# A decoder layer with routed experts: projections as three rounded products of split operands, quantised layers without diagonal matrices, routing in four pieces, and another order

## The chip, the core and the metric

The kernel runs on one core of one Trainium2 chip. The metric is the time of one execution on the device in microseconds (us). TensorE (PE) multiplies, VectorE (DVE), ScalarE (ACT) and GpSimd (POOL) work element by element, and SyncE (SP) issues the transfers between the device memory and the on-chip memory. The engines run side by side and wait for one another by semaphores. TensorE's clock has two levels, 1.2 and 2.4 GHz; a row of the profile gives the granted share of the higher one.

## The reference

Input x is four sequences of 512 tokens of width 512, all float32. One layer is three parts, each added to its input and normalised.

```
def attention(x, Wqkv, bqkv, Wo, bo):            # 16 heads of 32
    kqv = (x @ Wqkv + bqkv).reshape(b, s, 3, 16, 32)
    q, k, v = kqv[:, :, 0], kqv[:, :, 1], kqv[:, :, 2]
    scores = einsum('bsnh,btnh->bnst', k, q) / sqrt(32)
    scores = triu(scores) - 10000 * tril(ones, -1)
    attn = softmax(scores, axis=2)
    return einsum('bnkq,bknh->bqnh', attn, v).reshape(b, s, 512) @ Wo + bo

def quant_linear(x, w):                          # once per batch and layer
    s = sqrt(max|x| over tokens / max|w| over rows)      # one per input column
    xs, ws = x / s, w * s
    xq = round(xs / (max|xs| per row / 127)); wq = round(ws / (max|ws| per row / 127))
    return xq @ wq.T * x_scale * w_scale.T

x = layernorm(x + attention(x))
g, u = split(quant_linear(x, fside[b])); x = layernorm(x + quant_linear(silu(g) * u, ctx[b]))
x = layernorm(x + sum over 4 of 16 experts of their weighted FFN + 2 shared FFNs)
```

The routing takes the 2 best of 4 groups of experts and in them the 4 best experts, by ranks.

## The kernel before

**Stages.** A table of words, `SEQ`, gives the order of steps; every engine walks the same table and does its own part of each step. A first pass (from 0 to 148 us in the trace) does the attention (A) of batch 0. A loop of three turns does A of batch a together with the quantised layers and the routing (B) of batch a-1. Each turn ends with the output projection `wo`. A last pass does B of batch 3, mixed with halves of the shared experts' tiles (`half`), of which 8 tiles of 16 are merged into it. The other shared tiles follow, with the placing of tokens between them, then 71 or more tiles of the routed experts, and a last normalisation.

**Words of the table.** `xt` transposes x. `qk:n` and `v:n` are the projections, `max` the row maxima of the scores, `rows` turns the maxima into a row, `scores` the scores, exponentials and masks, `weigh` the weighted sum, `bc` divides by the denominators, `wo` is the output projection. For a quantised layer n, `wtr` and `xtr` transpose weights and inputs so that DVE can take column maxima, `s` makes the column scales, `ws` and `xs` bring a scale to all partitions and scale, `wq` and `xq` quantise, `wb` brings the weight scales to all partitions, `wqt` and `xqt` transpose, `h` multiplies. `ln1`, `a2` and `ln2` close the parts; `x2t`, `lg`, `lgt` and `route` are the routing.

**Products.** A projection step (`product`, L1097) is four float32 products of 512 columns, one for each 128 rows of the input width; the trace has two records for each. Weights lie in `room`, loaded once. The product by the diagonal matrices `dg` that DVE builds (L1609, L1617) brings a scale to all partitions (L1097 as well). The score products take q and k as a rounded part and a rest (`qhl`), which go through the device memory (`scr_d`) into stacked tiles `qst` and `kst`: SP stores them after each odd `qk`, waits, and loads six pieces of 256 KB (L680 to L690). `rows` sends two small rows, `nmh` and `nml`, into `qst` (L694, L695), and every fourth `scores` waits for them.

**Banks.** Three PSUM banks (`psR`) serve all one-bank steps in turn: a step waits until the step three tickets back has been read (`take_bank`). So the engine that reads a step's result also sets when PE may go on.

**What the queues hold.** SP's transfers go out in the order of its program. Per turn they are: fside and ctx of batch b (L653, L654), `xr` of batch a after the first normalisation of b (L660), `xt` of the next batch (L673), then the stores and loads of q and k, the rows, and `x2`.

## Time and profile before

| | us |
|---|---|
| median of 3 runs | 1494.71 |
| lowest and highest | 1491.39, 1494.90 |
| the profiled execution, as timed | 1494.37 |
| its span in the trace | 1492.6 |
| what lies around the span | 1.8 |

| engine | busy us | share |
|---|---|---|
| PE (TensorE) | 1337.6 | 90% |
| PEld (its weight loads, beside it) | 993.9 | 67% |
| DVE | 889.9 | 60% |
| ACT | 412.3 | 28% |
| POOL | 390.3 | 26% |

The shares are means over stages with different limits. The first row of a stage to read is the one that gives all engines in that stretch; then the waits of PE inside it. Busy time of PE is modelled, with matmuls that overlap.

### The profile page before, as it was taken

Reading aid. Unit: us, or ns where it says so; the run is one execution under the profiler, and the core shown is the slowest. Engines: PE = TensorE matmul, PEld = TensorE weight load, DVE = VectorE, ACT = ScalarE, POOL = GpSimd, SP = SyncE. Lnnn points to the kernel's source line nnn. Section 1 sums busy time; section 2 is a strip of 40 time slices with the busy share of each in tenths; the row PEclk is TensorE's granted clock in tenths of the full one; section 3 lists DMA queues with packets and bytes.
Section 4 is the critical chain, followed back from the end, with each engine's and each line's share of the span. In section 5 each row is a group of like instructions: output and inputs, shape, how many; then the busy total and the mean of one; then the engine's idle time right before and its main releaser. Section 6 shows DMA issues by size and latency. Waiting matters only on the chain.

```text
span 1492.6 us, 24655 instructions
## 1 busy us (share of the span) xinstructions
PE 1337.6 (90%) x7331; PEld 993.9 (67%) x7339; DVE 889.9 (60%) x1580; ACT 412.3 (28%) x628; POOL 390.3 (26%) x478
## 2 busy tenths in 40 slices
PE   7988998999999999689978997999999999879991
PEld 3553455445444554377867887899999999768891
DVE  2442787668866986786646876334343455455534
ACT  1131133313340234121120003223222334343423
POOL 1131012200230023000000671334343344243432
PEclk9989998999999999889998999999999999999996
DMA  8430533224422533203110012645464456868447
GB/s 281 131 93 34 155 97 89 72 100 126 114 71 73 153 105 128 90 14 110 64 57 29 29 43 64 164 75 130 86 140 76 86 131 138 236 159 247 80 78 248
DMA packets 90110, 163.98 MB, mean 110 GB/s; under 512 B 8544, under 2 KB 29536, under 8 KB 89968
## 3 DMA queue, kind: packets, MB, share of 16 engines
q1 hardware_dynamic: 73168, 122.88, 26.6%
q0 software_dynamic: 16816, 39.59, 14.3%
q8 instruction: 58, 0.95, 0.3%
q14 instruction: 68, 0.56, 0.1%
HBM read 113.42 MB, written 49.02 MB: 109 GB/s over the span
## 4 chain that ended last, share of the span: by engine, by line
PE 67%; DVE 13%; DMA 8%; issue 5%; ACT 3%; POOL 2%; SPq 1%; DVEq 1%; ACTq 0%; POOLq 0%
PE psR L1097 12%; PE psUA L1005 12%; PE psUB L1005 12%; PE psY L1012 9%; PE psR L1012 5%; PE psR L1173 3%; PE psOT L1204 3%; PE psST L1187 3%; PE psR L1111 2%; PE psTX L988 2%; DMA kst<-scr_d 2%; PE psTH L1021 2%; DMA room<-in_L_ffn_w_dram 2%; DMA qst<-nml 1%; DVE w_s L1261 1%
## 5 line engine op out<-in xcount | busy, mean ns | idle before, releaser
L1005 PE MATMUL psUA<-w_s,xgT 128*128 (+1 forms) x1284 | 246.5, 342 | 2.0 <-DVE xgT L1381 1.7
L1005 PE MATMUL psUB<-w_s,xgT 128*128 (+1 forms) x1284 | 226.8, 325 | 0.0
L1005 PEld LDWEIGHTS psUA<-w_s,xgT 128*128 128x128 f32 x1284 | 215.7, 197 | 9.7 <-issue 8.1
L1005 PEld LDWEIGHTS psUB<-w_s,xgT 128*128 128x128 f32 x1284 | 213.1, 191 | 0.0
L829 POOL DMA_INDIRECT sx_d<-yg,dst_i x74 | 119.5, 1614 | 304.5 <-ACT yg L908 265.7
L868 ACT ACTIVATE silg<-psUA 128x352 f32<-128x352 f32 x107 | 49.6, 464 | 444.0 <-PE psUB L1005 444.0
L1012 PE MATMUL psY<-w_s,hgT 128*128 (+3 forms) x621 | 161.4, 404 | 0.3 <-issue 0.3
L791 POOL TENSOR_SCALAR_AFFINE_SELECT pT<-pT 128x128 f32<-128x128 f32 (+1 forms) x192 | 68.7, 377 | 342.0 <-ACT pT L946 341.8
L1390 DVE SCALAR_TENSOR_TENSOR hg<-silg,cws,psUB 128x352 f32<-128x352 f32 x75 | 43.4, 579 | 176.3 <-ACT silg L868 176.3
L1571 DVE TENSOR_REDUCE nm<-psR 128x1 f32<-128x128 f32 (+3 forms) x256 | 112.4, 486 | 38.7 <-PE psR L1175 34.7
L1012 PEld LDWEIGHTS psY<-w_s,hgT 128*128 128x128 f32 (+1 forms) x621 | 113.4, 190 | 22.3 <-issue 0.5
L1097 PE MATMUL psR<-xT,room 128*128 128x512 f32 x256 | 117.4, 605 | 2.4 <-ACT xT L918 2.4
L1396 DVE CAST hgT<-psTH 128x384 fp32r<-128x384 f32 x107 | 59.5, 556 | 95.5 <-PE psTH L1021 95.1
L816 POOL DMA_INDIRECT xg<-x_d,src_i x77 | 98.4, 1279 | 52.9 <-issue 22.2
L1261 DVE TENSOR_TENSOR w_s<-room,w_s (+2 forms) x54 | 88.1, 1667 | 32.7 <-ACT w_s L859 31.9
L946 ACT ACTIVATE pT<-psST 128x512 f32<-128x512 f32 (+1 forms) x128 | 83.9, 703 | 85.5 <-PE psST L1187 84.6
L1173 PE MATMUL psR<-kst,qst 96*128 96x256 f32 (+2 forms) x256 | 91.4, 428 | 15.9 <-DMA kst<-scr_d 6.2
L1021 PE MATMUL psTH<-ident,hg 128*128 128x128 f32 x321 | 55.1, 281 | 39.9 <-DVE hg L1390 20.9
L1097 PEld LDWEIGHTS psR<-xT,room 128*128 128x128 f32 x256 | 48.1, 193 | 59.4 <-issue 54.5
L1012 PE MATMUL psR<-w_s,hgT 128*128 (+1 forms) x333 | 86.8, 405 | 1.0 <-issue 1.0
L1204 PE MATMUL psOT<-pT,v_s 128*32 128x256 f32 (+3 forms) x512 | 80.3, 440 | 7.4 <-POOL pT L791 7.4
L859 ACT CAST w_s<-room (+2 forms) x54 | 73.6, 1404 | 48.2 <-DVE room L1547 21.9
(221 smaller groups left out, 1923.3 us busy)
## 6 DMA issues: line engine op xcount, KB each, us to landing
room<-in_L_ffn_w_dram SPq DMA_DIRECT2D x32, 704.0 KB, 6.1
scr_d<-qhl SPq DMA_DIRECT2D x32, 512.0 KB, 3.7
qst<-scr_d SPq DMA_DIRECT2D x48, 256.0 KB, 3.9
kst<-scr_d SPq DMA_DIRECT2D x48, 256.0 KB, 5.8
room<-in_L_ffn_w_dram SPq DMA_DIRECT2D x16, 512.0 KB, 7.3
xt<-in_x_dram SPq DMA_DIRECT2D x5, 1024.0 KB, 7.2
xr<-in_x_dram SPq DMA_DIRECT2D x4, 1024.0 KB, 5.4
breg<-in_fside_BxS2xS_dram SPq DMA_DIRECT2D x4, 1024.0 KB, 7.6
```

The lines of the kernel that those rows point to most:

```text
L816: pool.indirect_dma_start(xg[:, par, :], None, x2_d, bass.IndirectOffsetOnAxis(ap=src_i[:, j:j + 1], axis=0)).then_inc(s_gat[par], 16)
L829: pool.indirect_dma_start(sx_d, bass.IndirectOffsetOnAxis(ap=dst_i[:, j:j + 1], axis=0), yg[:, par, :], None, compute_op=ALU.add).then_inc ...
L859: act.copy(hi, raw).then_inc(s_whi, 1)
L946: act.activation(pT[:, h % 4, lo:hi], psST[:, lo:hi], ACT.Exp, scale=SCALE).then_inc(s_exp, 1)
L1005: mm = pe.matmul(t[:, 0:F], xgT[:, par, a_, c * P:(c + 1) * P], w[:, buf, b_, c, :], start=(c == 0 and n == 0), stop=(c == C - 1 and n == ...
L1012: mm = pe.matmul(psy[:, :], hgT[0:kn, a_, k * P:(k + 1) * P], w2_s[0:kn, buf, b_, k, :], start=(first and k == 0 and n == 0), stop=(last_ ...
L1021: mm = pe.transpose(psTH[0:kn, k * P:(k + 1) * P], hg[:, k0:k0 + kn], ident[:, :])
L1097: mm = pe.matmul(out_, l, r, start=(n == 0), stop=(n == len(pairs) - 1))
L1173: pe.matmul(t[:, 0:w], qst[0:96, i, j, q * P:(q + 1) * P], kst[0:96, i, j, 0:w], start=True, stop=False)
L1204: pe.matmul(psOT[HD * j:HD * (j + 1), kb * P:S], v_s[:, kb, h * HD:(h + 1) * HD], pT[:, h % 4, cols], start=(kb == 0), stop=(kb == ST - 1) ...
L1261: dve.tensor_tensor(lo, raw, hi.bitcast(F32), ALU.subtract).then_inc(s_wlo if n in UP else s_w2lo, 1)
L1571: done(dve.tensor_reduce(nm[:, n, q:q + 1], at.bank(x, q)[:, 0:(q + 1) * P], AX.X, ALU.max, negate=True))
```

## The change

**Projections.** Weights of q, k, v and o are now kept as a rounded part and a rest (type fp32r), and so are x (`xT` has two halves) and the attention's output (`ohl`). A projection step is twelve rounded products instead of four float32 ones: high by high, high by low, low by high for each 128 rows. The split of a weight is made once, in the first pass: raw weights are loaded into tiles of B that are free then (`WRAW`), ACT copies the rounded part, DVE subtracts (`USES` says before which step). The tile `late_w` holds the q and k weights of groups 2 and 3 and later those of `wo`; both versions (128 x 4096 floats, 2 MB) are kept in the device memory and loaded again in every turn. DVE now makes the rest of each `xt` (ACT did the whole step before), ACT copies `v` (DVE added its bias before), and at `bc` ACT makes the rounded part and DVE the rest of the output, with the bias of v added there.

**Quantised layers.** The column maxima over the four row blocks are taken by DVE in one strided reduction (`largest`), so `wtr` and `xtr` transpose one block instead of four. Scales are brought to all partitions by transposing a broadcast column, without `dg`.

**Routing** is four steps, `route:0` to `route:3`, the last between `wo:2` and `wo:3`. **The order** in `SEQ` is another. In the last pass the halves are cut into `ha` (up) and `hb` (the rest), placed by a table, and the first weights' `split:0` stands ahead of `ln1`. **Memory:** fside shares its tile with `h1` and is loaded at the end of the turn before; `xg` has three buffers; two index tables are made by POOL at the start of the last pass.

```diff
@@ order of the steps, the start of the table
-            "xt:0 xt:1 xt:2 ln1 xt:3 wtr:0:0 qk:0 v:0 wtr:0:1 wtr:0:2 wtr:0:3 xtr:0:0 xtr:0:1 xtr:0:2 xtr:0:3 s:0 qk:1 "
...
+            "xt:0 xt:1 xt:2 xt:3 ln1 qk:0 wtr:0 v:0 xtr:0 s:0 qk:1 ws:0 v:1 wq:0 qk:2 qk:3 v:2 wb:0 max:0 wqt:0:0 "
...
+            "weigh:14 x2t:0 x2t:1 x2t:2 x2t:3 weigh:15 lg bc:0 bc:1 lgt bc:2 bc:3 route:0 route:1 route:2 wo:0 wo:1 "
+            "wo:2 route:3 wo:3 ").split()]
@@ which weight is split before which step
+        USES = {("qk", 0): 0, ("v", 0): 1, ("qk", 2): 2, ("qk", 4): 3, ("weigh", HEADS // 2): 4}
@@ SP
                 if a is not None:
                     if b is not None:
+
+                        sp.wait_ge(s_dfree, at.value(1, 0))
+                        apart(sp)
+                        sp.wait_ge(s_okept, 16)
+                        sp.dma_start(late_flat, late_d).then_inc(s_late, 16)
...
+                        if g == 2 and b is None:
+
+                            sp.wait_ge(s_wrest, TURN[3] + 1)
+                            sp.dma_start(late_d, late_flat).then_inc(s_wkept, 16)
+                        elif g == 3 and b is None:
+                            sp.wait_ge(s_wkept, 16)
+                            raw_part(4)
+                        elif g == 3:
+                            sp.dma_start(late_flat, wo_d).then_inc(s_wo, 16)
...
+                if a is not None and b is None:
+                    sp.wait_ge(s_wrest, TURN[4] + 1)
+                    sp.dma_start(wo_d, late_flat).then_inc(s_okept, 16)
+                if a is not None:
+                    sp.dma_start(wf[:, :, :], f_v[:, bass.ds(a, 1)]).then_inc(s_bw, 16)
+                    sp.dma_start(wc[:, :, :], c_v[:, bass.ds(a, 1)]).then_inc(s_bw, 16)
@@ PE
+            def three(l, r):
+
+                return [(l[0], r[0]), (l[0], r[1]), (l[1], r[0])]
...
-                        m = n // 2 + C * (n % 2)
-                        mm = product(t, [(wqkv[:, k, m * P:(m + 1) * P], xT[:, k, :]) for k in range(C)])
+                        g, m = divmod(n, 2)
+                        w_ = (early_qk, late_qk)[g // 2]
+                        mm = product(t, [x_ for k in range(C) for x_ in three(
+                            [w_[:, v, g % 2, k, m * P:(m + 1) * P] for v in range(2)], [xT[:, v, k, :] for v in range(2)])])
...
+                    elif kind in ("wtr", "xtr"):
+                        top = wm if kind == "wtr" else xm
+                        for m in range(C2 if n else C):
+                            mm = pe.transpose(t[:, m * P:(m + 1) * P], top[:, m * P:(m + 1) * P], ident[:, :])
+                    elif kind in ("ws", "xs", "wb"):
+                        col = {"ws": sm, "xs": rsm, "wb": wsc}[kind]
+                        for m in range(C2 if n and kind != "wb" else C):
+                            mm = pe.transpose(t[:, m * P:(m + 1) * P], col[:, m:m + 1].to_broadcast([P, P]), ident[:, :])
@@ DVE
+                def largest(top, src, signal):
+
+                    dve.tensor_reduce(top[:, 0:src.shape[2]], src.rearrange("p i n -> p n i"), AX.X, ALU.max,
+                                      apply_absolute_value=True).then_inc(signal, 1)
...
+                    if b is None and x in USES:
+                        w = USES[x]
+                        dve.wait_ge(s_wup, TURN[w] + 1)
+                        dve.tensor_tensor(WPART[1][w], WRAW[w], WPART[0][w].bitcast(F32),
+                                          ALU.subtract).then_inc(s_wrest, 1)
...
+                    elif kind == "xt":
+                        dve.wait_ge(s_xth, a * C + n + 1)
+                        done(dve.tensor_tensor(xT[:, 1, n, :], t, xT[:, 0, n, :].bitcast(F32), ALU.subtract))
...
                     elif kind == "ln1":
                         dve.wait_ge(s_dfree, at.freed(x))
-                        normalise(xr, s_qin)
+                        dve.wait_ge(s_bw, 32 * b + 32)
+                        normalise(xr, s_qin, lambda: largest(wm, wf, s_wm))
+                        after()
+                        apart(dve)
+                        dve.wait_ge(s_qin, 2 * b + 1)
+                        largest(xm, x1, s_xm)
@@ ACT
+                    if b is None and x in USES:
+                        w = USES[x]
+                        act.wait_ge(s_wld[w], 16 * (2, 1, 2, 4, 1)[w])
+                        act.copy(WPART[0][w], WRAW[w]).then_inc(s_wup, 1)
```

DVE at the start of a turn of the loop, before; `[waits ...]` names the semaphores.

```order
L1466 BN_STATS bn<-xr 128x6 [waits s_dfree]
L1466 BN_STATS bn<-xr 128x6 x3
L1455 ISA
L1470 BN_AGGR mv<-bn 128x2 [waits s_dve]
L1470 BN_AGGR mv<-bn 128x2 x3
L1455 REGISTER_ALU
L1472 TENSOR_SCALAR small<-mv 128x4 [waits s_dve]
L1462 ISA
L1475 TENSOR_SCALAR x<-xr,mv,small 128x512 [waits s_pow]
```

The same place now, from the last `xt` of the four on. The first TENSOR_REDUCE is `largest` over fside, the second over the normalised x.

```order
L1696 TENSOR_TENSOR xT<-psR,xT 128x512 [waits s_xth]
...
L1575 BN_STATS bn<-xr 128x6 [waits s_bw]
...
L1579 BN_AGGR mv<-bn 128x2 [waits s_dve]
...
L1594 TENSOR_REDUCE xs<-breg 128x512
L1571 ISA
L1586 TENSOR_SCALAR x<-xr,mv,small 128x512 [waits s_pow]
...
L1594 TENSOR_REDUCE xs<-x 128x512 [waits s_qin]
...
L1692 SCALAR_TENSOR_TENSOR qhl<-psR,bqk,qhl 128x512 [waits s_qkhi]
```

DVE now has four subtractions ahead of the first normalisation, and two reductions in it, all ahead of the rest of `qk:0`.

SP in a turn, the loads of group 3 and the rows of `rows:2`, before.

```order
L690 DMA qst<-scr_d 32x4x512 [waits s_st]
L690 DMA qst<-scr_d 32x4x512 x2
L690 DMA kst<-scr_d 32x4x512 x3
L239 REGISTER_ALU
L694 DMA qst<-nmh 1x16x128 [waits s_dfree]
L695 DMA qst<-nml 1x16x128
```

The same place now; `late_w<-wo_d` is the 2 MB of the output weights.

```order
L737 DMA qst<-scr_d 32x4x512 [waits s_st]
L737 DMA qst<-scr_d 32x4x512 x2
L737 DMA kst<-scr_d 32x4x512 x3
L746 DMA late_w<-wo_d 128x4096
L254 REGISTER_ALU
L750 DMA qst<-nmh 1x16x128 [waits s_dfree]
L751 DMA qst<-nml 1x16x128
```

The 2 MB have come to stand between the loads of k and the two small rows. In the first pass the store `late_d<-late_w`, also 2 MB, stands between the loads of group 2 and the rows of `rows:1`.

PE at the start of the first pass, before.

```order
L1111 MATMUL psR<-ident,xt 128x128 x3
L1097 MATMUL psR<-xT,room 128x512 [waits s_wqk,s_afree]
L1097 MATMUL psR<-xT,room 128x512 x3
L1097 MATMUL psR<-room,xT 128x512 [waits s_afree,s_wv]
L1097 MATMUL psR<-room,xT 128x512 x3
```

And now; `s_wrest` is DVE's subtraction for the weights of that step.

```order
L1202 MATMUL psR<-ident,xt 128x128 x3
L1188 MATMUL psR<-xT,early_w 128x512 [waits s_wrest,s_dfree]
L1188 MATMUL psR<-xT,early_w 128x512 x11
L1188 MATMUL psR<-wv_s,xT 128x512 [waits s_dfree,s_wrest]
L1188 MATMUL psR<-wv_s,xT 128x512 x11
```

Where PE waited for a load, it now waits for a load, a copy on ACT and a subtraction on DVE.

## Rows read from the trace of the kernel before

**Rows 1.** Windows by stage: us; busy PE, PEld, DVE, ACT, POOL; PEclk; DMA; GB/s
```profile
0.00:148.00 148.00, 127.93 (x608) 65.95 (x608) 51.79 (x97) 33.55 (x50) 27.05 (x83) 0.92 0.45 136
308.00:462.00 154.00, 141.91 (x762) 73.46 (x764) 119.57 (x238) 45.86 (x71) 26.50 (x56) 1.00 0.34 99
618.00:770.00 152.00, 124.67 (x694) 107.62 (x697) 103.63 (x184) 32.17 (x50) 3.72 (x4) 0.91 0.23 74
```
**Rows 2.** Chain of waits (start us, us, what), rounded products and float32 transposes
```profile
975.87 2.10 PE psY L1012 x9
318.68 4.24 PE psR L1111 x28
```
**Rows 3.** Timeline of PE in the second turn, float32 products and a diagonal one
```profile
337.55 1.02 PE L1097 MATMUL psR<-dg,ones 128*128 128x512 f32 x2
338.41 3.60 PE L1097 MATMUL psR<-room,xT 128*128 128x512 f32 x8
342.15 0.39 PE L1173 MATMUL psR<-kst,qst 96*128 96x256 f32 x1
```
**Rows 4.** Timeline of DVE: starts of turns 1 and 3, and single operations
```profile
147.95 2.47 DVE L1466 BATCH_NORM_STATS2 bn<-xr 128x6 f32<-128x512 f32 x4
461.76 0.69 DVE L1586 TENSOR_TENSOR xr<-xr,psR 128x512 f32<-128x512 f32 x1 [2.60 <-PE psR L1097]
465.84 2.47 DVE L1466 BATCH_NORM_STATS2 bn<-xr 128x6 f32<-128x512 f32 x4 [3.39 <-issue]
475.66 2.47 DVE L1592 TENSOR_REDUCE amx<-psR 128x1 f32<-128x512 f32 x4
481.85 0.75 DVE L1562 SCALAR_TENSOR_TENSOR qhl<-psR,bqk,qhl 128x512 fp32r<-128x512 f32 x1
487.34 2.29 DVE L1487 TENSOR_REDUCE amw<-xs 128x4 f32<-128x2048 f32 x1
385.95 1.22 DVE L1487 TENSOR_REDUCE amw<-xs 128x4 f32<-128x1024 f32 x1
```
**Rows 5.** Timeline of PE and SP in the first pass
```profile
13.48 3.67 PE L1097 MATMUL psR<-xT,room 128*128 128x512 f32 x8 [0.72 <-ACT xT L918]
25.62 0.88 SPq L680 DMA_DIRECT2D scr_d<-qhl  x2
38.48 0.38 PE L1173 MATMUL psR<-kst,qst 96*128 96x256 f32 x1 [0.73 <-DMA kst<-scr_d]
```
**Rows 6.** Timeline of SP and PE: a small row, and who waits for it
```profile
384.25 0.59 SPq L695 DMA_DIRECT2D qst<-nml  x1
389.07 0.90 PE L1187 MATMUL psST<-qst,kst 98*128 98x512 f32 x4 [0.98 <-DMA qst<-nml]
```
**Rows 7.** DMA issues: KB each, median us from issue to landing
```profile
qst<-nml SPq DMA_DIRECT2D x16, 8.0 KB, 1.8
```
**Rows 8.** Windows while xr and xt, 2 MB, are loaded; columns as in 1
```profile
322.00:324.00 2.00, 2.00 (x10) 1.17 (x9) 2.00 (x4) 0.00 (x0) 0.00 (x0) 1.00 1.03 386
```
**Rows 9.** Timeline of PE at the end of the second turn, three steps of `wo`
```profile
445.55 10.56 PE L1097 MATMUL psR<-room,otu 128*128 128x512 f32 x24 [1.00 <-DVE otu L1583]
```
**Rows 10.** Timeline of ACT in the second turn: a copy of 512 columns, four times
```profile
309.22 2.05 ACT L918 COPY xT<-psR 128x512 f32<-128x512 f32 x4 [19.54 <-PE psR L1111]
```
**Rows 11.** Windows of PE, first pass: us; busy (x); granted clock; DMA; GB/s
```profile
124.00:128.00 4.00, 2.39 (x3) 0.63 0.00 0
128.00:132.00 4.00, 4.00 (x6) 0.52 0.00 0
```
**Rows 12.** Timeline of the last pass: its start on DVE, and waits of PE
```profile
617.22 0.69 DVE L1586 TENSOR_TENSOR xr<-xr,psR 128x512 f32<-128x512 f32 x1 [4.29 <-PE psR L1097]
631.42 1.12 PE L1111 MATMUL psR<-ident,breg 128*128 128x128 f32 x4 [8.77 <-DVE amw L1592]
646.56 0.90 PE L1021 MATMUL psTH<-ident,hg 128*128 128x128 f32 x3 [5.79 <-DVE hg L1386]
751.13 0.90 PE L1021 MATMUL psTH<-ident,hg 128*128 128x128 f32 x3 [4.17 <-DVE hg L1386]
```

418 lines of the change are left out of this document (240 added, 178 removed), and 18 rows, old and new, of tables (SEQ, ending).

## The prediction

> **What bounds the kernel now.** I read the windows by stage first [rows 1]. In a turn of the loop PE is busy for 141.9 of 154.0 us at full clock, DVE for 119.6: PE is the bound, and its waits are the remaining 12 us. In the first pass PE has 127.9 of 148.0 us at a mean clock of 0.92, in the last pass 124.7 of 152.0 at 0.91. So about 20 and 27 us there are waits. Everything from 770 us on (shared rest, routed tiles) keeps its products, and only its buffers change; I cost it at nothing, within 3 us either way.
>
> **PE's work.** A rounded product of 512 columns takes 2.10/9 = 0.233 us and a float32 transpose of 128 columns 4.24/28 = 0.151 us [rows 2]. A projection step of four float32 products has 8 records in 3.60 us, of which some 3.43 us is its spacing without the last overlap; twelve rounded ones should take 12 x 0.233 = 2.80 us, 0.63 less. Eight steps `qk`, four `v` and four `wo` per batch give 10.1 us. In `wtr` and `xtr` one block is transposed instead of four: 36 transposes fewer per batch, 36 x 0.151 = 5.5 us. A diagonal product of two records is 1.02 us [rows 3] against 4 transposes, 0.6 us: over the 20 column blocks about 1.3 us. Together 16.9 us of PE per batch, 68 us in four batches. If PE's busy time were the whole story, that would be the gain. Most of it I expect to turn into waits.
>
> **DVE's work** stays equal. Per batch it loses 12 column reductions of 2.47/4 = 0.62 us [rows 4] (7.4), the additions of v (2.5) and the diagonal tiles (4.2): 14.1. It gains four rests of x and four of the output at about 0.65 us (5.2), and `largest` twice over 2048 and twice over 1024 elements. The contiguous reductions of those sizes take 2.29 and 1.22 us [rows 4], so 7.0 us, and four short reductions 2.0: 14.2. What changes is where this work stands.
>
> **The start of a turn** is counted from the end of the last addition of `wo` on DVE. The second turn begins so at 308.25 us, since 342.15 is the first score product of `max:0` [rows 3] and lies 33.9 us behind it. In that stretch PE works nearly without a pause, on transposes, projections and `s`. DVE had slack: after the branch back it stood 3.39 us ("issue") ahead of its first statistics at 465.84, while the entry at 147.95 shows none [rows 4], and nobody waited. Now DVE's four rests of x stand ahead of `qk:0`, so the 3.4 us count. Then come rests 2.6, statistics 3.2, a reduction 2.3 over the power on POOL, scaling 1.9 and a reduction 2.3: 15.9 us from the start. The rest of `qk:0` at 0.75 follows, the two short reductions, the scales (19.9), and the rest of `qk:1` ends at 21.4. From that rest to the first product of `max:0` the first pass took 38.48 - 25.6 = 12.9 us (two stores, a wait, six loads) [rows 5]. So `max:0` comes at 34.2 us instead of 33.9. All that PE saves here (seven steps, 24 transposes, the scales: 9 us) becomes waiting.
>
> From `max:0` on, five projection steps give back 3.1 us; of this I keep 2.2, for `xq:1` and `rows:2` now stand close together on DVE. Then SP's queue: the 2 MB `late_w<-wo_d` go out right ahead of the rows of `rows:2`. A row sent right behind the loads of k, at 384.25, released PE at 389.07, after 4.8 us [rows 6], where the median landing is 1.8 us [rows 7]: bytes queued ahead delay a small row. At 386 GB/s [rows 8] 2 MB take 5.4 us. Half of these lie beside `weigh:4` to `weigh:7` and `max:12`; I take 3 us of waiting ahead of `scores:8`, between 0 and 6. The Trainium skill (DMA: Bandwidth & Descriptors, Queues, rings and completion order) says that each DMA engine consumes descriptors in ring order, but that completion is not first-in first-out for an issuing engine. The first half is the sum above; by the second a row could overtake, and the 3 us would be nothing.
>
> At the end, three steps of `wo` took 10.56 us [rows 9]. Four save 2.5 us, but ACT and DVE each have a part of every `bc` now and `route:3` sits between two `wo`: +1.9, net -0.6. A turn comes to +0.3 - 2.2 + 3.0 - 0.6 = +0.5; PE's waits at its start can lower the clock (below), for which I add 0.5. **Three turns: +3 us**, between -12 (no queue delay, the start hides less) and +15.
>
> **The first pass.** Today PE's first step starts at 13.48, 0.72 us behind ACT [rows 5]. Now the weights of `qk:0` need a copy on ACT (1024 elements) and a subtraction on DVE. A copy of 512 took 2.05/4 = 0.51 us [rows 10], so 1.0, and the subtraction is about 1.2: +2.9 with the rests of x. `v:0` waits for 2048 elements: 2.1 on ACT and 2.3 on DVE, some 5.2 us in all with what is ahead of them. Against this stand three steps at 0.63. The rest of `qk:1` goes from 25.6 to about 31.5, `max:0` +5.8. The third split (weights of groups 2 and 3, 4096 elements in two) costs another 2.3, three steps give back 1.9: +6.2. The 2 MB store `late_d<-late_w` ahead of the rows of `rows:1` has nothing beside it, since there is no layer B here: +6 (between 0 and 7). `wo` gives -2.5, its split weights and the split outputs +2. Waits also cost clock: after a window in which PE was busy for 2.39 of 4 us, the granted clock was 0.63 and then 0.52, the lower level [rows 11], so its products took double. **Sum about +12**, between +3 and +20.
>
> **The last pass** [rows 12]. From the end of `wo` (617.91) PE's transposes of `wtr` start only at 631.42, 8.77 us of them waiting for DVE. Now `split:0`, `lead` and a half with 6.5 us of products stand ahead. ln1 moves back by DVE's 4.8 us split, so I take -3.6, between 0 and -6.5. Products give -2.6 here (no projections, only the transposes and scales). Two waits, 5.79 and 4.17 us for `hg`, are met by the cutting into `ha` and `hb`, which puts other work in between: -3.8 together. Against it the routing has only `hb:7:1` beside it: +3. **Sum -7**, between -14 and 0.
>
> **The forecast.** The profiled execution took 1494.37 us, 0.3 below the median 1494.71. 1494.4 + 12 + 3 - 7 = 1502.4; I forecast **1502 us**, 0.5% slower. About 0.3% (4.5 us) is what a measurement of this kernel can tell from no change.
>
> **Rivals.**
> First, *the small rows are not held up, and the clock holds*. Rows 7 speaks for it (8 KB land in 1.8 us), rows 6 against it. Three turns then lose 9 us of queue and 1.5 us of clock, the first pass 6: 1502 - 16 = 1486. Chance 0.22.
>
> Second, *PE stays the bound throughout*: the start of a turn follows PE because DVE's order is not strict there in effect (rests short, ACT's copies early). Rows 1 (142 of 154) speaks for it; the strict order of DVE's words and the 12.9 us behind `qk:1` against it. It gives up to 16.9 in each turn and in the last pass a little: 1494 - 40 = 1454, between 1432 and 1475. Chance 0.12.
>
> Third, *the strided reductions are slow*, on the slower side. `largest` steps through four row blocks, 2 KB or 1 KB apart, for every result. The trace only has contiguous ones (2.29 us for 2048), so it does not bound this from above; I bound it by double. Two of them (2.3 us more each) then stand ahead of the rest of `qk:0`, and 2.4 us more of layer 1 lie ahead of `s:1`: +7 per batch, of which nothing is hidden in the turns and most is hidden in the last pass: 1502 + 3 x 7 + 3 = 1526. It decides from about 3.5 us per `largest`. Chance 0.12. The Trainium skill (SBUF — State Buffer, its note on SBUF cachelines) says that each access that crosses to a new 16-byte line pays a penalty, and that float32 can stride over four elements for free; by that this rival would be the case. No row of before has a strided operand of this kind that shows it.
>
> Fourth, the splits and stores of the first pass cost more, with half clock in the long stretches: 1515 to 1522. Chance 0.06. The forecast with its own range, 1494 to 1512, has 0.48.
>
> **How the numbers follow.** The range takes in the first and the fourth rival, the forecast's bounds and the point of the third: 1478 to 1526. It leaves out the second (0.12) and half of the third. Faster by over 0.3% (below 1490.2): 0.12 + 0.20 = 0.32. Within 0.3%: 0.02 of the first and 0.14 of the forecast's lower end, 0.16. Slower (above 1499.2): 0.34 + 0.12 + 0.06 = 0.52.
>
> **What the profile after would show.** Projection steps of twelve records in 2.8 us. In a turn, `max:0` 34 us behind the end of `wo`, with PE waiting for `qhl` or `kst` in that stretch; if it comes at 27 to 30, the second rival is right. PE waiting 2 to 4 us for `qst<-nmh` or `nml` at `scores:8`; none would be the first. `largest` at 2.3 and 1.2 us; at 4.6 it is the third. The first pass ending near 160, a turn still at 154 to 155, the last pass near 145. The forecast falls if a turn changes by more than 3 us, and most likely it would fall at the start of a turn, since the order of DVE's work there decides 9 us in each.

## The result, and the profile after

The changed kernel is slower: 1523.84 us, the median of 4 runs (1521.02 to 1534.76), against 1494.81 for the kernel before on the same chip, ratio 1.0218, interval 1.0181 to 1.0256. That is 29 us where 7 were forecast. The sign was right; 1502 us lies below the whole interval. The stated range, 1478 to 1526, does hold the measured time, but only because its upper end is the point of the third rival (slow strided reductions), whose cause turned out to make 6 to 9 us of the 24 it was given: that the range holds is luck.

The spans are 1492.6 and 1523.1 us, 30.5 apart. Counted from the end of the last addition of `wo` on DVE, as in the prediction:

| stretch | before | after | difference | forecast |
|---|---|---|---|---|
| first pass | 147.9 | 171.7 | +23.8 | +12 |
| first turn | 160.3 | 161.5 | +1.2 | +1 |
| second turn | 154.2 | 161.9 | +7.7 | +1 |
| third turn | 155.5 | 166.2 | +10.7 | +1 |
| last pass and rest | 874.7 | 861.9 | -12.8 | -7 |

The windows by stage of the changed kernel answer to [rows 1]; they are the first pass, the second turn and the last pass.

```profile
core 0: us, PE busy (x) PEld busy (x) DVE busy (x) ACT busy (x) POOL busy (x), PEclk, DMA share, GB/s
0.00:172.00 172.00, 130.97 (x673) 86.84 (x673) 64.27 (x105) 46.29 (x63) 27.55 (x80) 0.83 0.47 140
333.00:495.00 162.00, 136.88 (x800) 90.59 (x800) 125.05 (x218) 50.99 (x79) 26.91 (x56) 0.89 0.41 121
661.00:810.00 149.00, 127.45 (x722) 111.84 (x723) 105.91 (x165) 30.90 (x50) 5.57 (x8) 0.90 0.25 81
```

In the second turn PE was busy for 141.9 of 154 us at clock 1.00; now it is busy for 136.9 of 162 at 0.89. PE's work fell by 17 us by the prediction's sum, but its busy time by only 5: the mean clock of 0.89 means that some of the work was done at the lower level, where it takes longer. DVE's busy time rose by 5.5 us (119.6 to 125.1), of which the slower reductions below make 4.3. The windows of PE at the start of the second turn show how it goes (us; busy; granted clock; DMA; GB/s).

```profile
333.00:337.00 4.00, 2.15 (x16) 1.00 0.72 223
337.00:341.00 4.00, 2.28 (x8) 0.83 0.72 305
341.00:345.00 4.00, 2.34 (x6) 0.74 0.00 0
345.00:349.00 4.00, 3.57 (x13) 0.68 0.15 15
369.00:373.00 4.00, 2.39 (x10) 0.67 0.84 284
373.00:377.00 4.00, 4.00 (x22) 0.50 0.79 174
377.00:381.00 4.00, 4.00 (x18) 0.50 1.06 215
```

PE is first busy for little more than half of each window, then the clock falls to the lower level; it falls again after the wait for `kst`. The timeline of PE there, with the idle time ahead of each group and what ended it:

```profile
333.45 1.52 PE L1202 MATMUL psR<-ident,xt 128*128 128x128 f32 x12 [1.86 <-DVE xr L1721]
336.37 0.66 PE L1202 MATMUL psR<-ident,xt 128*128 128x128 f32 x4 [1.40 <-DVE xT L1696]
338.75 4.59 PE L1188 MATMUL psR<-xT,early_w 128*128 128x512 f32 x12 [1.72 <-DVE xT L1696]
345.43 0.65 PE L1330 MATMUL psR<-ident,xs 128*128 128x128 f32 x4 [2.09 <-DVE xs L1594]
351.61 0.66 PE L1330 MATMUL psR<-ident,xs 128*128 128x128 f32 x4 [1.19 <-DVE qhl L1692]
352.20 3.02 PE L1188 MATMUL psR<-xT,early_w 128*128 128x512 f32 x12
370.61 0.58 PE L1277 MATMUL psR<-kst,qst 96*128 96x256 f32 x1 [3.23 <-DMA kst<-scr_d]
```

Twelve rounded products take 3.02 us at full clock, as forecast with 2.8, but 4.59 in the first step, more than the 3.60 of the float32 ones in [rows 3]. `max:0` starts 37.4 us after 333.17, where 34.2 was forecast and 33.9 stood before. DVE's timeline gives the 3 us:

```profile
338.50 2.47 DVE L1575 BATCH_NORM_STATS2 bn<-xr 128x6 f32<-128x512 f32 x4
341.62 3.67 DVE L1594 TENSOR_REDUCE xs<-breg 128x512 f32<-128x2048 f32 x1
345.21 1.90 DVE L1586 TENSOR_SCALAR x<-xr,mv,small 128x512 f32<-128x512 f32 x4
347.15 3.74 DVE L1594 TENSOR_REDUCE xs<-x 128x512 f32<-128x2048 f32 x1
```

A strided reduction of 2048 elements takes 3.67 to 3.74 us, where the contiguous one in [rows 4] took 2.29. The Trainium skill (SBUF — State Buffer, its note on SBUF cachelines) has a penalty for such strides; the trace agrees in kind, with 1.6 times, not double.

The first pass, PE:

```profile
16.25 5.46 PE L1188 MATMUL psR<-xT,early_w 128*128 128x512 f32 x12 [2.97 <-DVE early_w L1669]
26.60 3.78 PE L1188 MATMUL psR<-wv_s,xT 128*128 128x512 f32 x8 [4.89 <-DVE wv_s L1669]
40.73 5.73 PE L1188 MATMUL psR<-xT,early_w 128*128 128x512 f32 x24 [2.88 <-DVE early_w L1669]
50.59 0.38 PE L1277 MATMUL psR<-kst,qst 96*128 96x256 f32 x1 [1.32 <-DMA kst<-scr_d]
61.86 5.19 PE L1188 MATMUL psR<-xT,late_w 128*128 128x512 f32 x12 [2.98 <-DVE late_w L1669]
96.17 1.54 PE L1291 MATMUL psST<-qst,kst 98*128 98x512 f32 x4 [7.29 <-DMA qst<-nml]
```

Every wait of the prediction is there: the start at 16.25 (+2.8 against [rows 5]; forecast +2.9), 4.89 us for `v:0`, 7.29 us for the small row behind the 2 MB store (+6). What is not in the sum is the clock: behind four of these waits PE runs at half speed (5.46 and 5.19 us for twelve products, 3.78 for eight, 1.54 for the four score products); only behind the wait at 40.73 it does not (24 in 5.73 us). The rows of the clock show 1.00 at 16.25 all the same; that the step was slow is read from its 5.46 us, against 3.31 in the run warm below. `max:0` is at 50.59, 12.1 us late instead of 5.8.

In the turn the chain of waits shows the other small row, from its issue on:

```profile
437.13 7.00 DMA qst<-nml
444.25 1.54 PE psST L1291 x4
```

It took 7.00 us behind the 2 MB of `late_w<-wo_d`, against 4.8 in [rows 6] and 1.8 in [rows 7]. The Trainium skill (DMA: Bandwidth & Descriptors, Queues, rings and completion order) says that each DMA engine takes descriptors in ring order; both traces agree, and no overtaking is seen: here the 2 MB, issued at 431.16, landed after 12.6 us, and the row 0.4 us behind them. But most of the 7 us lay beside other work: PE waited 2.81 us for `kst` at `max:12` and only 1.54 us here, and then worked at 0.50. In the other two turns the wait for this row was 0.61 and 0.92 us, so 1.0 on the mean where 3 were forecast.

### The profile page after: what moved, and what is told of

It reads as the page before. It is cut to its first block, busy times and chain, and to the rows that moved or that the text cites. A ratio compares the mean times of both kernels' runs of the same rounds, so it can differ in the third digit from the quotient of the medians.

```text
span 1523.1 us, 24966 instructions
## 1 busy us (share of the span) xinstructions
PE 1316.6 (86%) x7483; PEld 1058.9 (70%) x7483; DVE 917.2 (60%) x1504; ACT 439.7 (29%) x664; POOL 394.1 (26%) x479
## 4 chain that ended last, share of the span: by engine, by line
PE 64%; DVE 16%; DMA 8%; issue 5%; ACT 2%; SPq 2%; DVEq 1%; POOL 0%; ACTq 0%; POOLq 0%
PE psUA L1090 12%; PE psUB L1090 12%; PE psY L1097 9%; PE psR L1188 7%; PE psR L1097 5%; PE psR L1277 4%; PE psST L1291 3%; PE psOT L1308 3%; PE psTX L1073 2%; DMA kst<-scr_d 2%; PE psTH L1106 2%; DMA qst<-nml 2%; DMA room<-in_L_ffn_w_dram 2%; DVE xs L1594 2%; PE psR L1202 1%
## 5 line engine op out<-in xcount | busy, mean ns | idle before, releaser
L1090 PEld LDWEIGHTS psUA<-w_s,xgT 128*128 128x128 f32 x1284 | 215.0, 198 | 25.9 <-DVE xgT L1491 15.3
L1700 DVE TENSOR_REDUCE nm<-psR 128x1 f32<-128x128 f32 (+3 forms) x256 | 117.3, 488 | 77.4 <-PE psR L1279 70.0
L1277 PE MATMUL psR<-kst,qst 96*128 96x256 f32 (+2 forms) x256 | 112.2, 514 | 30.4 <-DMA kst<-scr_d 22.5
L1370 DVE TENSOR_TENSOR w_s<-room,w_s (+2 forms) x54 | 88.1, 1666 | 32.0 <-ACT w_s L931 30.5
L1277 PEld LDWEIGHTS psR<-kst,qst 96*128 96x128 f32 x256 | 67.6, 264 | 41.7 <-issue 24.6
L1312 PE MATMUL psDEN<-pT,hot 128*32 128x256 f32 (+3 forms) x512 | 81.2, 448 | 0.0
## 6 DMA issues: line engine op xcount, KB each, us to landing
late_w<-wo_d SPq DMA_DIRECT2D x3, 2048.0 KB, 12.6
```

The source lines that it names most:

```text
L1090: mm = pe.matmul(t[:, 0:F], xgT[:, par, a_, c * P:(c + 1) * P], w[:, buf, b_, c, :], start=(c == 0 and n == 0), stop=(c == C - 1 and n == ...
L1277: pe.matmul(t[:, 0:w], qst[0:96, i, j, q * P:(q + 1) * P], kst[0:96, i, j, 0:w], start=True, stop=False)
L1312: mm = pe.matmul(psDEN[q0:q0 + HD, kb * P:S], hot[:, g, :], pT[:, h % 4, cols], start=(g == 0 and kb == 0), stop=(g == C - 1 and kb == ST ...
L1370: dve.tensor_tensor(lo, raw, hi.bitcast(F32), ALU.subtract).then_inc(s_wlo if n in UP else s_w2lo, 1)
L1700: done(dve.tensor_reduce(nm[:, n, q:q + 1], at.bank(x, q)[:, 0:(q + 1) * P], AX.X, ALU.max, negate=True))
```

## The experiments

Ratios are to the kernel before on the same chip, with their 95% interval, and the changed kernel's is 1.0218. 1% is 15 us. Stretches are from the profiled executions.

### What the clock costs: unread products at the waits

```diff
+            def warm(x, a, b):
+                first = {("qk", 0): 3, ("v", 0): 5, ("qk", 2): 3, ("max", 0): 1, ("qk", 4): 3, ("scores", 4): 8,
+                         ("max", 12): 3, ("bc", 0): 3, ("wo", 0): 2}
+                turn = {("xt", 0): 2, ("xt", 3): 1, ("qk", 0): 2, ("wtr", 0): 4, ("xtr", 0): 3, ("max", 0): 3,
+                        ("max", 12): 3, ("scores", 8): 1, ("wo", 0): 2}
...
+                for _ in range(n_):
+                    pe.matmul(t_, ident[:, :], sel[:, :, :].rearrange("p n q -> p (n q)"), start=True, stop=True)
```

> The changed kernel with products that nobody reads (the unit matrix by sel, 512 columns float32, into a bank that is free there) put ahead of the steps at which PE waits: 31 in the first pass (qk:0, v:0, qk:2, max:0, qk:4, scores:4, max:12, bc:0, wo:0) and 21 in a turn (xt:0, xt:3, qk:0, wtr:0, xtr:0, max:0, max:12, scores:8, wo:0). Nothing is left out. Theory C (the waits themselves are small, what costs is that the clock falls behind them): the granted clock of the first pass and the turns rises from 0.83 to 0.89 to 0.95 or more, and each pass gets 5 to 12 us shorter, 1480 to 1505 against 1524 on the chip of the first measurement. Theory D (the path runs over DVE and the transfers there, PE at half clock only fills its waits): the clock rises and the time does not, within 5 us of the changed kernel, or longer by what the products overrun their waits.

Measured: 1495.1 us, ratio 0.9996 (0.9964 to 1.0028). The whole loss is gone, and nothing else of the change was touched. First pass 155.5 us (from 171.7), turns 159.5, 160.0 and 159.0. The mean granted clock is 0.96 in the first pass and in each turn (0.83, 0.89, 0.89 and 0.86 in the changed kernel). The windows of PE at the start of the second turn, to be held against those above:

```profile
315.00:319.00 4.00, 4.00 (x23) 1.00 0.73 236
319.00:323.00 4.00, 4.00 (x15) 1.00 0.70 293
323.00:327.00 4.00, 3.99 (x11) 1.00 0.00 0
327.00:331.00 4.00, 3.66 (x17) 1.00 0.26 12
371.00:375.00 4.00, 2.44 (x17) 0.91 0.37 137
375.00:379.00 4.00, 4.00 (x19) 0.50 0.00 0
```

The engine does work that nobody needs, and the clock stays at its higher level until 371 us; at a place where no such products stand and PE is busy for 2.44 of 4 us, it falls. That is why theory C holds and D does not. The gain doesn't come at `max:0`, which starts 37.6 us behind the start of this turn, as before (37.4): up to there DVE and the transfers set the pace. It comes behind it: `scores:0` starts at 54.9 instead of 58.3 us. The two parts alone:

```diff
-                turn = {("xt", 0): 2, ("xt", 3): 1, ("qk", 0): 2, ("wtr", 0): 4, ("xtr", 0): 3, ("max", 0): 3,
-                         ("max", 12): 3, ("scores", 8): 1, ("wo", 0): 2}
+                turn = {}
```

That is warmfirst; in warmturn `first = {}` and `turn` is that of warm.

> The changed kernel with the unread products of warm in the first pass alone (31). Nothing is left out. In warm the first pass was 16 us shorter and the three turns 11 us together. If the parts add: 16 us below the changed kernel, ratio 1.010 to 1.013. Rival (the turns' state of the clock depends on how the pass before ends, so that the turns change too): ratio below 1.006 or above 1.017.

> The changed kernel with the unread products of warm in the turns alone (21 in each). Nothing is left out. If the parts add: 11 to 14 us below the changed kernel, ratio 1.011 to 1.015, with turns of 159 to 160 us and a first pass of 170 to 172. Rival (the turns gain nothing by the clock, since DVE and the transfers are their path): ratio 1.019 to 1.023.

Measured: 1.0117 (1.0069 to 1.0166) and 1.0104 (1.0045 to 1.0163), gains of 15 and 17 us, which add up to the 33 of warm. So the first pass and the turns lost about the same to the clock; each of the two gains is uncertain by some 9 to 10 us. Single stretches of a profile are less sure than these ratios: the turns of warmfirst, with no product in them, are 165.2, 167.0 and 163.4 us where the changed kernel's are 161.5, 161.9 and 166.2, and the first pass of warmturn, also untouched, is 164.2 us instead of 171.7. In pairs, oldend and ln1late (all below), whose first pass is untouched as well, it is 168.0, 168.1 and 166.7, so the 171.7 is the longest of five. Where the clock falls depends on small shifts, and a stretch by itself tells only of differences above some 7 us.

The same products in the kernel before, 9 in its first pass and 5 in a turn:

```diff
+                first = {("qk", 0): 1, ("max", 0): 1, ("scores", 4): 1, ("max", 12): 2, ("bc", 0): 3, ("wo", 0): 1}
+                turn = {("xt", 0): 1, ("scores", 4): 1, ("max", 12): 1, ("scores", 8): 1, ("wo", 0): 1}
```

> The kernel before with unread products at its own few waits: 9 in the first pass (qk:0, max:0, scores:4, max:12, bc:0, wo:0) and 5 in a turn (xt:0, scores:4, max:12, scores:8, wo:0). Nothing is left out. Its half-clock stretches are 43 to 50, 96 to 107 and 125 to 131 us in the first pass, 249 to 262 and 301 to 307 in the first turn. Theory C: they shrink and it takes 1480 to 1488, ratio 0.990 to 0.997, so that the change without its clock losses would still be the slower kernel. Rival (before hardly loses clock): 1490 to 1496, ratio 1.00.

Measured: 1.0019 (0.9994 to 1.0045). Its first pass became 9 us shorter (138.9), its turns 6 us longer in all (475.9 against 470.0). Where PE hardly waits and the clock is up (0.96 to 1.00 in those turns of before), unread products look like mere extra work, though 6 us in one profile is within the scatter of stretches. Theory C's gain for before did not come. The two kernels with such products can't be told apart (0.9996 and 1.0019).

### The first pass: splits ahead of their use

```diff
+        SPLITS = {("qk", 0): (0, 1), ("v", 0): (2,), ("v", 1): (3,), ("weigh", HEADS // 2): (4,)}
...
-                    if b is None and x in USES:
-                        w = USES[x]
+                    for w in SPLITS.get(x, ()) if b is None else ():
```

> The changed kernel with each weight split one or two steps ahead of its use in the first pass: the split for v:0 before the rest of qk:0, that for qk:2 before v:0, that for qk:4 before v:1. Nothing is left out. Theory P (the first pass loses its time to the chain copy on ACT, subtraction on DVE, each started only at its step, and to half clock behind those waits): the 4.9, 2.9 and 3.0 us waits shrink, with the clock 8 to 14 us less, 1510 to 1516. Theory D (the raw weights arrive only just then): under 2 us less, 1522 to 1524.

Measured: 1.0132 (1.0082 to 1.0182), 13 us less; the first pass is 156.6 us instead of 171.7. Its timeline of PE:

```profile
16.25 5.28 PE L1188 MATMUL psR<-xT,early_w 128*128 128x512 f32 x12 [2.97 <-DVE early_w L1668]
21.36 2.96 PE L1188 MATMUL psR<-wv_s,xT 128*128 128x512 f32 x12
```

`v:0` follows `qk:0` without a pause: the raw weights had been there, and only the place of copy and subtraction in the order of ACT and DVE held them up. That refutes theory D. How much of the 13 us is the waits and how much the clock behind them, this run does not tell (see bestnoq below).

### SP's queue: the 2 MB behind the rows

```diff
-                        if g == 2 and b is None:
...
-                        elif g == 3:
-                            sp.dma_start(late_flat, wo_d).then_inc(s_wo, 16)
...
                         sp.dma_start(qst[97:98, i].bitcast(F32), nml[:, i, :].bitcast(F32)).then_inc(s_mrow[i], 16)
+                        if x[1] == 1 and b is None:
+                            sp.wait_ge(s_wrest, TURN[3] + 1)
+                            sp.dma_start(late_d, late_flat).then_inc(s_wkept, 16)
+                        elif x[1] == 2 and b is not None:
+                            sp.dma_start(late_flat, wo_d).then_inc(s_wo, 16)
```

> The changed kernel with its two 2 MB transfers one place later in SP's queue: late_w<-wo_d behind the two rows of rows:2 instead of ahead of them, late_d<-late_w behind the rows of rows:1. Nothing is left out. Theory W (a wait of PE costs its own length and then some 12 us at half clock): the waits at scores:8 (about 3 us of 3 turns) and at scores:4 of the first pass (7.3 us) vanish with the half-clock stretches behind them, 25 to 35 us less than the changed kernel, so 1490 to 1499. Theory Q (only the waits themselves count): 9 + 7 = 16 us less, 1508. Theory N (the rows are not held up by the 2 MB): no change, 1524.

Measured: 1.0121 (1.0055 to 1.0187), 14.5 us less. That is theory Q's number, but with the two intervals it is anything from 3 to 26 us, and theory Q's shares are not borne out: the first pass is 159.9 us, 11.8 shorter, though PE's wait at `scores:4` fell by only 4.9 (2.42 us instead of 7.29), while the three turns are 489.2 us instead of 489.6 together. The waits for the row at `scores:8` are gone, but they were 0.61, 1.54 and 0.92 us; those for `kst` at `max:12`, 2.7 to 2.8 us, are still there. The 3 us per turn of the prediction did not show in the time. With the clock held up (best, below, against the same kernel with the transfers back at their places):

```diff
-                        if x[1] == 1 and b is None:
...
-                            sp.dma_start(late_flat, wo_d).then_inc(s_wo, 16)
...
-                first = {("qk", 0): 3, ("max", 0): 6, ("scores", 4): 2, ("max", 12): 3, ("bc", 0): 3, ("wo", 0): 2}
+                first = {("qk", 0): 3, ("max", 0): 6, ("scores", 4): 8, ("max", 12): 3, ("bc", 0): 3, ("wo", 0): 2}
```

> best with the two 2 MB transfers back at their places ahead of the rows, and 8 instead of 2 unread products at scores:4 of the first pass. Nothing is left out. Theory Q (5 to 7 us of wait in the first pass, 1 to 3 in each turn): 8 to 14 us above best, ratio 0.994 to 0.999. Rival (in the turns the rows are not held up to a point that matters): 5 to 7 us, ratio 0.992 to 0.994.

Measured: 1.0012 (0.9986 to 1.0037) against 0.989 for best, 18 us, more than either number. In the profiles 3.8 of 15.3 us are in the first pass, 5.7 in the turns and 5.8 behind them, where the kernels are equal. That the transfers cost something in the turns is likely by this; how much stays open. This run is also warm with the splits of early (and fewer products in the first pass), and it stands at 1.0012 where warm stands at 0.9996: with the clock held up the place of the splits gains nothing in the whole time that can be told from noise. Its first pass is 11.3 us shorter than warm's in the profile, and the rest is longer by 12.

### The stride

```diff
-                    dve.tensor_reduce(top[:, 0:src.shape[2]], src.rearrange("p i n -> p n i"), AX.X, ALU.max,
+                    dve.tensor_reduce(top[:, 0:src.shape[2]].rearrange("p (i m) -> p i m", i=ST),
+                                      src.rearrange("p i (m j) -> p i m j", j=ST), AX.X, ALU.max,
```

> The changed kernel with the same column reductions made over four neighbouring elements instead of over four row blocks (it takes the maxima of other elements, so the scales are other ones; the count of elements and instructions is the same). Theory S (the stride is what makes a reduction of 2048 take 3.7 instead of 2.3 us, and this lies ahead of the rests of qk:0 and qk:1): largest at 2.3 us, max:0 of a turn 2.8 us earlier, 3 turns 8 us less plus up to 6 us of clock, 1510 to 1516. Theory T (the time is that of 512 results with their own overhead, not of the stride): largest stays at 3.7 and nothing changes, 1524.

> warm and pairs together: the unread products at the waits, and the column reductions over neighbouring elements (other maxima, same count). With the clock held up the price of the stride should show by itself. Theory S: it lies on the path at the start of every turn, 2.8 us, and partly in layer 1 and in the last pass: 8 to 12 us below warm, ratio 0.992 to 0.995. Rival (what is gained at max:0 is lost again before scores:3, as in pairs with the lower clock): ratio 0.997 to 1.001.

Measured: pairs 1.0177 (1.0131 to 1.0223), warmpairs 0.9937 (0.991 to 0.9965), 6 and 9 us less than their bases. In warmpairs DVE's timeline has

```profile
162.59 2.28 DVE L1611 TENSOR_REDUCE xs<-breg 128x512 f32<-128x2048 f32 x1
166.73 2.29 DVE L1611 TENSOR_REDUCE xs<-x 128x512 f32<-128x2048 f32 x1
227.91 1.21 DVE L1611 TENSOR_REDUCE xs<-breg 128x256 f32<-128x1024 f32 x1
```

and the turns are 158.7, 156.3 and 157.0 us, 6.5 shorter together than in warm. The interval of pairs overlaps that of the changed kernel, and that of warmpairs just touches that of warm, so neither run alone is clear of noise; both point the same way, and the size is less sure than the direction. In pairs `max:0` starts 34.2, 34.9 and 34.7 us behind the start of the turn (36.4, 37.4 and 37.3 in the changed kernel), as the prediction had it with contiguous reductions (34.2). As many results, as many elements: it is the stride, 1.4 us each, and two of them lie on the path of every turn. With 472.0 us these three turns are within 2 us of the 470.0 before.

### What the rounded products are worth

```diff
-                        mm = product(t, [x_ for k in range(C) for x_ in three(
-                            [w_[:, v, g % 2, k, m * P:(m + 1) * P] for v in range(2)], [xT[:, v, k, :] for v in range(2)])])
+                        mm = product(t, [(w_[:, 0, g % 2, k, m * P:(m + 1) * P].bitcast(F32), xT[:, 0, k, :].bitcast(F32))
+                                         for k in range(C)])
...
```

The steps `v` and `wo` are changed in the same way.

> The changed kernel with four float32 products of the rounded parts in each qk, v and wo instead of the twelve rounded ones; the rests are still made but not used (so the projections lack the products of the rests). All else as changed. It undoes the PE side of the first part of the change. If PE's time were the bound, 16 steps x 0.63 us x 4 batches = 40 us more. Theory H (PE has waits at the start of a turn, 7 of 16 steps hide there): 15 to 25 us more. Theory K (longer products keep PE busy and the clock up, which gives back what they cost): 0 to 10 us more, with a granted clock above 0.89 in the turns.

> best with four float32 products of the rounded parts in each qk, v and wo instead of twelve rounded ones (the rests are made and not used). All 64 steps are 0.63 us longer for PE, 40 us. Theory H (behind the waits at a turn's start 7 of 16 steps hide, in the first pass fewer): 18 to 25 us above best, ratio 1.001 to 1.006. Rival (with the clock held up PE is the bound nearly everywhere): 30 to 40 us, ratio 1.009 to 1.016. Rival (12 us as between four and the changed kernel): ratio 0.997.

Measured: four 1.0302 (1.0275 to 1.0329), 12.5 us more than the changed kernel; bestfour 1.0019 (0.9991 to 1.0048), 19 us more than best. Of 40 us of PE a third to a half reaches the time. Where is less clear. In the profiles of best and bestfour the first pass makes 12.8 us of it and the three turns make nothing (480.4 and 479.7 us); in those of four and the changed kernel the turns make 12.4 (502.0 and 489.6) and the first pass 7.1. In the second and third turn of bestfour the granted clock is 1.00 and PE is busy for 151.2 and 150.1 of 158 us; in best it is 0.96, with 148 of 160. So with the shorter products part of the saving in a turn goes into waits and part into the lower clock that stands beside them, and how the rest divides stays open.

### The two orders

> The changed kernel with the order of the steps of the kernel before (wtr:0 and xtr:0 as one step at the place of their first, the four parts of route ahead of wo:0). Nothing is left out. It undoes the part on the order of the turns; ln1 stands between xt:2 and xt:3 there, so it is ahead of the last rest of x and of qk:0. Theory O (the new order is better by what it saves between max:0 and wo): 3 to 8 us per turn more. Rival (the order makes no difference, the waits at the start of a turn and the clock do): within 5 us of the changed kernel. If ln1 ahead of xt:3 holds the projections up, max:0 comes 2 to 6 us later than 37 us from the start.

```diff
-            "xt:0 xt:1 xt:2 xt:3 ln1 qk:0 wtr:0 v:0 xtr:0 s:0 qk:1 ws:0 v:1 wq:0 qk:2 qk:3 v:2 wb:0 max:0 wqt:0:0 "
+            "xt:0 xt:1 xt:2 ln1 xt:3 wtr:0 qk:0 v:0 xtr:0 s:0 qk:1 "
+            "v:1 ws:0 qk:2 wq:0 qk:3 wb:0 v:2 max:0 max:1 wqt:0:0 wqt:0:1 max:2 wqt:0:2 wqt:0:3 max:3 xs:0 qk:4 rows:0 "
```

Measured: 1.0616 (1.0594 to 1.0638), 59 us more; turns of 183.0, 184.5 and 184.1 us, `max:0` at 42.9 to 44.0 from their start and `scores:15` 17 to 22 us late. The old order doesn't go with the new steps: the rest of `xt:3` stands behind all of `ln1` on DVE (in the second turn at 366.18, 17 us behind its start), and PE waits 7.47 us for `largest` and 5.21 for that rest before `qk:0`. The prediction took the order as neutral; by itself it is worth 60 us here.

> The changed kernel with the last pass in the order of the kernel before: ln1 ahead of split:0 and lead, each half in one piece at its old place, two halves behind lgt. Nothing is left out. From the end of the last wo to the first routed tile the kernel before took 322.0 us, the changed one 312.0. Theory E (the new order of the last pass makes all of the 10 us): 322 us in that stretch, 8 to 12 us slower than the changed kernel, 1532 to 1536 against 1524. Rival (the 10 us come from fewer transposes and products without diagonals, some 3 to 5 us, and the rest from the order): 4 to 7 us slower.

```diff
-            "split:0 lead ln1 ha:0:0 hb:0:0 wtr:0 split:1 xtr:0 "
+            "ln1 split:0 wtr:0 lead xtr:0 s:0 split:1 ha:0:0 hb:0:0 ws:0 ha:0:1 hb:0:1 wq:0 wb:0 ha:1:0 hb:1:0 "
```

Measured: 1.0271 (1.0237 to 1.0304), 8 us more. From the end of the last `wo` to the end it is 872.5 us in the profile, against 861.9 in the changed kernel and 874.7 before. So the order of the last pass makes 8 to 10.6 of the 12.8 us gained there; the 2.2 that are left for fewer transposes and no diagonals are within the scatter.

Then the prediction's own suspect, `ln1` ahead of the projections:

```diff
-            "xt:0 xt:1 xt:2 xt:3 ln1 qk:0 wtr:0 v:0 xtr:0 s:0 qk:1 ws:0 v:1 wq:0 qk:2 qk:3 v:2 wb:0 max:0 wqt:0:0 "
+            "xt:0 xt:1 xt:2 xt:3 qk:0 v:0 qk:1 ln1 v:1 qk:2 wtr:0 xtr:0 s:0 qk:3 ws:0 v:2 max:0 wq:0 wb:0 wqt:0:0 "
```

> The changed kernel with one line of its order changed: qk:0, v:0 and qk:1 stand ahead of ln1, wtr:0, xtr:0 and s:0, max:0 ahead of wq:0. Nothing is left out. Theory L (DVE's ln1 ahead of the rests of qk is what makes PE wait at a turn's start and lowers its clock): the rest of qk:1 ends some 10 us earlier, max:0 at 27 to 30 us from the turn's start instead of 37, the granted clock there stays at 1.00; 5 to 10 us less per turn, 1494 to 1509. Theory R (DVE as a whole has too little slack, 125 of 162 us, so what is taken from the start comes back before h:0): under 2 us per turn, 1518 to 1526.

Measured: 1.057 (1.0521 to 1.062), 52 us more, and neither theory had that: `max:0` starts at 46.0 to 47.6 us. The rest of `qk:1` is indeed ready 17.2 us after the start of the second turn, but SP's own queue stands in between:

```profile
375.78 0.38 SPq L707 DMA_DIRECT2D xr<-in_x_dram  x1
376.54 0.37 SPq L720 DMA_DIRECT2D xt<-in_x_dram  x1
377.02 1.22 SPq L727 DMA_DIRECT2D scr_d<-qhl  x2
387.49 1.28 SPq L737 DMA_DIRECT2D qst<-scr_d  x3
```

`xr` waits for the end of `ln1`, and the stores of q and k, whose data were there at 366.8, stand behind it; then they follow 2 MB of `xr` and `xt`, so that the loads go out 10.5 us later. So I moved those two loads behind the loads of `qk:1`, with the 2 MB transfers as in queue:

```diff
-                        sp.wait_ge(s_qin, 2 * b + 1)
-                        apart(sp)
-                    sp.dma_start(xr[:, :, :], x_v[:, bass.ds(a, 1)]).then_inc(s_xr, 16)
...
+                        if g == 0 and b is not None:
+                            sp.dma_start(xt[:, :, :], x_v[:, bass.ds((a + 1) % B, 1)]).then_inc(s_x, 16)
+                            sp.wait_ge(s_qin, 2 * b + 1)
+                            apart(sp)
+                            sp.dma_start(xr[:, :, :], x_v[:, bass.ds(a, 1)]).then_inc(s_xr, 16)
```

> ln1late (qk:0, v:0, qk:1 ahead of ln1) with the two loads that stood ahead of the first store of q and k in SP's queue, xr (which waits for the end of ln1) and xt, put behind the loads of qk:1, and the two 2 MB transfers as in queue. Nothing is left out. ln1late was 52 us slower; in its trace the store of qk:1 went out 10 us after its rest, right behind xr. Theory S (SP's queue behind ln1 was the cost, and without it the early projections pay): max:0 at 27 to 32 us from a turn's start, 1490 to 1505. Theory B (banks and the order of DVE's other steps cost as well): max:0 early but scores:0 not earlier than 58 us, 1515 or more.

Measured: 1.0299 (1.0277 to 1.0322), 40 us less than ln1late (some 14 of them may be the transfers, as in queue), but 27 above queue, its base. `max:0` is at 35.5 to 37.6, hardly earlier than in queue (36.7 to 38.8), so theory B missed there as well, and `scores:0` only at 63.1 to 65.2 (56 to 60 in queue). The loads of `qk:1` now go out 21 us behind the start of the turn, but PE waits 3.00 and 4.83 us for the two reductions (transposes of layer B stand ahead of `max:0`), then 2.19 for the row maxima and 4.57 for `xq:0`, all of them DVE's. That fits theory B's cause: DVE's steps, not one of them, are what the start of a turn goes by. Putting `ln1` later gains nothing.

### All that paid, together

The edits of early, queue and warm, with 19 instead of 31 unread products in the first pass, since some of its waits are shorter:

```diff
-                first = {("qk", 0): 3, ("v", 0): 5, ("qk", 2): 3, ("max", 0): 1, ("qk", 4): 3, ("scores", 4): 8,
-                         ("max", 12): 3, ("bc", 0): 3, ("wo", 0): 2}
+                first = {("qk", 0): 3, ("max", 0): 6, ("scores", 4): 2, ("max", 12): 3, ("bc", 0): 3, ("wo", 0): 2}
```

> The changed kernel with three of the edits together: the splits one or two steps ahead of their use (early), the two 2 MB transfers behind the rows (queue), and the unread products at the waits that are left (warm; in the first pass none at v:0, qk:2, qk:4, 6 at max:0, 2 at scores:4). Nothing is left out. Theory C (the waits of the first pass and the clock are separate losses): 12 us of the first pass below warm, 1478 to 1486 on the chip where before takes 1493, ratio 0.990 to 0.995. Rival (warm already holds all that there is, since early and queue gained mostly clock): 1488 to 1495, ratio 1.00.

Measured: 1478.59 us, ratio 0.989 (0.9859 to 0.9921): 1.1% faster than the kernel before and 3.2% faster than the changed one. The first pass is 140.4 us, 7.5 below before, the turns 480.4 (470.0 before), last pass and rest 857.2 (874.7 before). Against warm it is 16 us less. By the whole times these come with the transfers (bestnoq, 18 us), not with the splits; the profiles put most of them into the first pass (155.5 to 140.4).

## Why the prediction was wrong

The reading of the windows by stage, the price of a rounded product and the start of a turn as the place where PE's saving vanishes were right; with contiguous reductions (pairs) even the 34.2 us of `max:0` are met. DVE's work was to stay equal, and did but for the stride. The steps one by one:

- **The clock is the step that failed.** For a turn it took 0.5 us ("PE's waits at its start can lower the clock"), for the first pass the remark that products then take double, inside a sum that left it out. Measured by warm, warmfirst and warmturn: 15 us in the first pass, 17 in the turns (5.6 each), 33 together, as much as the whole loss. With the clock held up (warm) the kernel is 8 us below the forecast. The prediction had counted the waits at a turn's start itself (9 us of saving turned into waiting) and had [rows 11] for what follows them, and did not multiply. In [rows 1] the clock of 1.00 in a turn belonged to a PE that was busy for 142 of 154 us, and it was taken over into a plan in which it waits.
- **The stride** was a rival with 0.12, at double. It is 1.6 times, and costs 6 us (pairs) to 9 us (warmpairs). Its price was known only from contiguous rows, and those were taken as the value instead of as the lower end.
- **The first pass**, +12 against +23.8. Its waits came about as forecast (2.97, 4.89, 7.29 us), and the clock behind them is what the sum left out. In the profiles early is 15.1 us shorter there, queue 11.8 and warm 16.2; they overlap, since best, which has all three, is 31.3 us shorter. The untouched first passes of other runs, 164.2 to 168.1 us, say that some 4 us or more of each of these are scatter.
- **The queue in the turns**: the mechanism is there (7.00 us for a small row), but PE's waits for it were 0.61, 1.54 and 0.92 us, not 3 each; they are not in the time of queue, and only unclearly in bestnoq.
- **The last pass**, -7 against -12.8: its order gives 8 us by the ratios and 10.6 in the profile of oldend, where the prediction's terms for it come to -4.4. For fewer products 2.6 were forecast and 2.2 are left, which one profile can't confirm.
- **The turns' remaining steps.** After clock and stride are taken out, three turns are about as long as before (472.0 against 470.0, and with 21 unread products in each). The prediction had +0.5 per turn there. Only the sum agrees: its term for the queue was three times too large, and those for `max:0` onwards and for `wo` were not measured singly, so that is partly luck.

The first rival (the small rows are not held up and the clock holds, 1486) was wrong on the clock, and on the rows in the first pass; in the turns PE hardly waited for them. The second (PE stays the bound) had its own sign, `max:0` at 27 to 30 us; it came at 36.4 to 37.4. The third came within 3 us of the measured time (1526) and its sign, a `largest` of over 3.5 us, was met, yet it isn't the cause of the time: it is worth 6 to 9 us, and warm, which keeps the stride, has none of the loss. The fourth (0.06, half clock in the long stretches, 1515 to 1522) named the cause, but for the first pass alone.

## What to carry to other kernels

Where a change takes work off an engine that is the bound and adds a dependency ahead of it, cost the waits at the clock that they leave behind: find in the trace what the granted clock does behind a wait of that length, and charge the work behind it at that level. Products that nobody reads, put into such waits, are a quick test of how much of a loss is clock, and here also the cheapest repair; where the engine is already busy they cost what they take. Before steps are moved on one engine, look at what its partner's queue has in front of the transfer that the moved step feeds.

## What the runs showed of the hardware

- At the start of the second turn PE was busy for 2.15, 2.28 and 2.34 us of three windows of 4, and the granted clock went from 1.00 to 0.83, 0.74 and 0.68, so partly to the level of 1.2 GHz; with products in the gaps (3.66 to 4.00 of 4) it kept 2.4 GHz at the same place. The whole effect, 33 us, was as large as the loss.
- A maximum over 2048 float32 elements in steps of 2 KB takes 3.7 us on DVE, over neighbours 2.29; over 1024 in steps of 1 KB 1.95 against 1.21.
- A row of 8 KB issued behind 2 MB landed after 7.00 us, where the median is 1.8 [rows 7]; moving the 2 MB behind it in SP's queue gained 14.5 us (3 to 26) of the whole time.
